# Vision tower kernel: who issues the upper halves of x's blocks 5, 6 and 7

## What is computed

```python
h = tok(x, W)              # windows of 16 steps at stride 8 (edge padding 8), rfft of each,
                           # real and imaginary parts times W: (8, 1024, 64)
f = h / norm(h)
s = softmax(f @ f.T) @ f   # over all 8192 tokens
a = f * 0.8 + s * 0.2;  a = a / norm(a)
h = layernorm(h + a)
h = layernorm(h + moe(h))  # 8 experts, the best 2 of each token, gelu: h + sum of gated experts
```

## Time and profile before

| What | Value |
|---|---|
| Time, median of 2 runs | 871.58 us (871.42 to 871.73) |
| Profiled execution: its own time | 872.53 us |
| Profiled execution: its span | 870.7 us |
| TensorE busy | 850.0 us (98%) |
| VectorE busy | 782.9 us (90%) |
| ScalarE busy | 660.2 us (76%) |
| GpSimd busy | 183.3 us (21%) |
| Mean granted TensorE clock | 0.994 |
| Moved by DMA | 26.50 MB |

### The profile page before, as it was taken

How to read it: one execution, slowest core, us unless ns; L and a number is a source line. 1 busy time by engine, 2 the same in 40 slices (tenths; PEclk the granted TensorE clock), 3 DMA queues, 4 the chain that set the end, 5 groups by cost and what they waited for, 6 DMA issues and landing times.

```text
span 870.7 us, 31169 instructions
## 1 busy us (share of the span) xinstructions
PE 850.0 (98%) x13498; PEld 438.8 (50%) x13498; DVE 782.9 (90%) x929; ACT 660.2 (76%) x1315; POOL 183.3 (21%) x187
## 2 busy tenths in 40 slices
PE   7989999999999999999999999999999999999995
PEld 6434556655555555555555555555555555543331
DVE  5677999998999899989998998899989999989994
ACT  0168888887888787878887888788878778878873
POOL 1066730000310000000000000000000299948323
PEclk9999999999999999999999999999999999999998
DMA  9984041000000000000000000000000000000111
GB/s 282 324 228 88 12 93 15 3 3 2 3 2 2 3 2 3 2 3 3 2 4 2 2 3 3 3 2 3 3 2 3 3 2 3 3 1 2 35 28 37
DMA packets 31784, 26.50 MB, mean 30 GB/s; under 512 B 12576, under 2 KB 29472, under 8 KB 31648
## 3 DMA queue, kind: packets, MB, share of 16 engines
q1 hardware_dynamic: 22768, 15.38, 7.3%
q10 hardware_dynamic: 8752, 8.86, 3.5%
q0 software_dynamic: 128, 0.26, 0.1%
HBM read 18.21 MB, written 2.10 MB: 23 GB/s over the span
## 4 chain that ended last, share of the span: by engine, by line
PE 93%; DVE 2%; ACT 2%; issue 2%; DMA 0%; POOLq 0%; DVEq 0%; ACTq 0%; POOL 0%
PE ps L532 38%; PE ps L549 26%; PE ps L562 13%; PE ps L631 3%; PE ps L714 3%; PE ps L575 2%; PE ps L449 2%; PE ps L463 1%; ACT ring L943 1%; PE ps L453 1%; PE ps L437 1%; DVE ring L1232 1%; PE ps L643 1%; PE ps L439 1%; ACT ring L906 0%
## 5 line engine op out<-in xcount | busy, mean ns | idle before, releaser
L1066 DVE TENSOR_TENSOR ring<-ring 128x1024 f16<-128x1024 f32 x512 | 605.0, 1232 | 41.1 <-ACT ring L943 40.1
L943 ACT ACTIVATE ring<-ps 128x1024 f32<-128x1024 f32 x512 | 519.7, 1021 | 128.7 <-PE ps L532 128.4
L532 PE MATMUL ps<-big 64*64 64x512 f16 x6144 | 376.3, 376 | 1.3 <-ACT ring L943 0.9
L549 PE MATMUL ps<-ring,both_f 64*64 64x512 bf16 x4096 | 275.3, 384 | 0.0
L532 PEld LDWEIGHTS ps<-big 64*64 64x64 f16 x6144 | 176.1, 106 | 159.5 <-ACT ring L943 5.5
L549 PEld LDWEIGHTS ps<-ring,both_f 64*64 64x64 f16 x4096 | 119.1, 106 | 106.8
L562 PE MATMUL ps<-ring,both_f 64*64 64x512 f16 x2048 | 154.3, 376 | 0.1
L943 ACT ACTIVATION_READ_ACCUMULATOR ring<-ps 128x1 f32 x512 | 101.2, 198 | 0.0
L376 POOL TENSOR_SCALAR stat<-stat 128x16 f32<-128x16 f32 (+2 forms) x4 | 1.9, 467 | 449.7 <-DVE stat L1115 449.4
L562 PEld LDWEIGHTS ps<-ring,both_f 64*64 64x64 f16 x2048 | 59.7, 107 | 51.9 <-issue 1.9
L906 ACT ACTIVATE ring<-ps,b1s 128x512 f32<-128x512 f32 x64 | 40.4, 683 | 17.5 <-PE ps L631 17.4
(11 more groups left out here) (181 smaller groups left out, 581.1 us busy)
## 6 DMA issues: line engine op xcount, KB each, us to landing
ring<-in_x_dram ACTq DMA_DIRECT2D x6, 1024.0 KB, 19.5
ring<-in_x_dram SPq DMA_DIRECT2D x6, 1024.0 KB, 19.9
big<-big SPq DMA_DIRECT2D x16, 128.0 KB, 2.5
out_dram<-h SPq DMA_DIRECT2D x14, 128.0 KB, 2.4
both_f<-in_x_dram SPq DMA_DIRECT2D x1, 1024.0 KB, 25.4
big<-in_x_dram SPq DMA_DIRECT2D x1, 1024.0 KB, 28.2
both_f<-in_x_dram ACTq DMA_DIRECT2D x1, 1024.0 KB, 20.6
big<-in_x_dram ACTq DMA_DIRECT2D x1, 1024.0 KB, 24.9
```

The source lines that it names most:

```text
L532: last = mm(bank(SLOT_BANK[slot_of(s)] + r)[m:m + 64, :], of_k[r][:, 128 * k + m:128 * k + m + 64], of_q[r][:, q0 + 512 * r:q0 + 512 * r + ...
L549: last = mm(bank(sums_bank(s // NT) + half)[m:m + 64, :], fs[64 * r:64 * r + 64, s % NT, m:m + 64], probs[64 * r:64 * r + 64, s % 8, :].bi ...
L943: a(probs[:, s % 8, :], bank(SLOT_BANK[slot_of(s)], 2), ACT.Exp, accum_out=rowsum[:, s:s + 1]).then_inc(s_pr, 1)
L1066: tt(probs_lo[:, s % 8, :], probs[:, s % 8, :], probs[:, s % 8, :].bitcast(BF16)[:, 1:2 * QC:2], ALU.subtract).then_inc(s_lo, 1)
```

## The change

The loop on ScalarE no longer loads blocks 5, 6 and 7. GpSimd issues these three upper halves, after its cast of `sel` and before its first inverse norm, each after the same count of `s_prod` as before. They count on three semaphores of their own, `s_xp`, since `s_xc` would otherwise be raised from two engines; the two places that wait for the upper half wait for `s_xc` (blocks 0 to 4) or `s_xp` (blocks 5 to 7), each for 16. The lower halves and all other work stay as they were.

```diff
--- before.py
+++ after.py
@@ -225,6 +225,7 @@
 
         s_cst, s_self, s_wg, s_xe, s_w, s_w1r = (sem(n) for n in ("s_cst", "s_self", "s_wg", "s_xe", "s_w", "s_w1r"))
         s_xb = [sem(f"s_x{i}") for i in range(XR)]
+        s_xp = [sem(f"s_xp{i}") for i in range(3)]
         s_xc = [sem(f"s_xc{i}") for i in range(XR)]
         s_hilo = [sem(f"s_hilo{i}") for i in range(2)]
         s_lohi = [sem(f"s_lohi{i}") for i in range(2)]
@@ -327,6 +328,10 @@
             nc.gpsimd.tensor_copy(ident16[:, :], ident).then_inc(s_id16, 1)
             pool.wait_ge(s_self, 32)
             nc.gpsimd.tensor_copy(sel[:, :], sel_f).then_inc(s_id16, 1)
+            for b in X_BEHIND:
+                pool.wait_ge(s_prod, X_BEHIND[b])
+                pool.dma_start(x_at(b)[64:128, 0:NM].rearrange("p m s v -> p m (s v)"),
+                               x_h[b, 1]).then_inc(s_xp[b - 5], 16)
             gt, pool_ts = nc.gpsimd.tensor_tensor, nc.gpsimd.tensor_scalar
 
             def sl(n):
@@ -456,7 +461,7 @@
 
             def loaded(b):
                 pe.wait_ge(s_xb[X_SLOT[b]], 16 * X_TURN[b])
-                pe.wait_ge(s_xc[X_SLOT[b]], 16 * X_TURN[b])
+                pe.wait_ge(s_xc[b] if b < 5 else s_xp[b - 5], 16)
 
             def kept_busy(n):
                 for i in range(n):
@@ -803,9 +808,6 @@
                 edge(b)
             for b in range(B):
                 act.wait_ge(s_prod, b + 1)
-                for later in X_BEHIND:
-                    if X_BEHIND[later] == b + 1:
-                        load(later)
                 used = 12 if b >= 2 else 8
                 a(prod[:, b // 2, 0:used, b % 2, :], bank(2 * (b % 2), 2)[:, 0:V * used].rearrange("p (k v) -> p k v", v=V),
                   ACT.Copy).then_inc(s_prodev, 1)
@@ -1015,7 +1017,7 @@
 
                 if s == SHARED_TAPS[b][0]:
                     dve.wait_ge(s_xb[X_SLOT[b]], 16 * X_TURN[b])
-                    dve.wait_ge(s_xc[X_SLOT[b]], 16 * X_TURN[b])
+                    dve.wait_ge(s_xc[b] if b < 5 else s_xp[b - 5], 16)
                     dve.wait_ge(s_edge, b - 1)
                 if (b - 1, s) in SHARED:
                     dve.wait_ge(s_taken, SHARED.index((b - 1, s)) + 1)
```

## The result

The changed kernel takes 884.89 us (median of 2 runs, 884.64 to 885.15), the kernel before 871.58. The ratio is 1.0154, with a 95% interval of 1.0137 to 1.0170: 13.3 us slower. The profiled execution took 885.15 us at a span of 883.3. The forecast was slower by 4.6 us, 876.2, with a range of 868.5 to 880. The direction was right and so was the place, the landing of block 4; the forecast loss was a third of what came, and the time lies above the range.

The account below looks back on a forecast made before the run. TensorE bounds the steady part; in the head, ScalarE's issue stalls delay block 4. Crowding by GpSimd's packets would start block 4 at 50.4 instead of 45.79, clock unchanged: 871.6 + 4.6 = 876.2 us, range 868.5 to 880.

Parts of the forecast that it names:

- What bounds the head, and the stall: First 75 us: ScalarE's 5.79 us issues delay block 4; removal worth 3.8 + 1.75 = 5.5 us if x were there.
- 0.3 for block 5: Block 5 landing at 47.4 against 47.1 wanted would take back at most 0.3 us of the gain.
- GpSimd's issues and the cover behind them: GpSimd's three issues take 1.7 us each; even at 5.79, the delayed inverse norm is barely covered by ScalarE's 2.88 us idle.
- The packets: Queues alternate by packet; GpSimd's 4 KB against 1 KB take two thirds of the rate, starting 4.8 us after issue.
- The landing of block 4: GpSimd's 3.15 MB pass first at 348 GB/s, 9.0 us: block 4 lands at 50.4, starting 4.6 us late.
- the loads behind block 4: After 50.4, block 5's lower half needs 3.0 us at 348 GB/s, landing at 53.4; nothing else is late.
- The fifth rival: Slow clock lasts through blocks 4 and 5, or one 1 KB-packet queue misses 348 GB/s: above 880 us; chance 0.06.
- The clock: TensorE around block 4: same 1.75 us slow-clock cost as before, no difference; bounds a gain or loss of 1.75.
- No crowding: GpSimd's packets of x do not hold up block 4; the 5.5 us less 0.3 is gained: 866.4 us; chance 0.13.
- equal shares: GpSimd's packets of x are 1 KB, each queue gets 116 GB/s, block 4 lands at 44.5: 869.8 us; chance 0.13.
- the stall only moves: GpSimd's queue fills, its issues take 5.79 us or more and delay the inverse norms: 871.6 us; chance 0.06.

Follow-up runs that it names:

- in another way: Kernel before, with ScalarE issuing block 6's half behind its b = 1 copies and block 7's behind the squares of h 0 and 1: 867.65 us, 0.9944.
- The transfers alone: Separate kernel, computing nothing of the reference: only loads of x in eleven successive phases, varying queues and partition halves; 204 to 213 GB/s into one half, 347 to 351 into both.
- the run with blocks 6 and 7: Changed kernel, but GpSimd issues only the upper halves of blocks 6 and 7 and ScalarE block 5's: 879.78 us, 1.0086 of the kernel before.
- the one with SyncE alone: Changed kernel, but SyncE instead of GpSimd issues the upper halves of blocks 5 to 7, each behind its lower half: 880.07 us, 1.0090 of the kernel before.
- the ninth phase: Phase of the loads-only kernel with SyncE loading the lower half, ScalarE and GpSimd the upper, the changed kernel's mix: 253 GB/s.
- the fifth phase: Phase of the loads-only kernel with GpSimd alone loading the upper half of the partitions: 213 GB/s.

## Why the prediction was right or wrong

**What bounds the head, and the stall: right.** The issues of 5.79 us were the chain, and taking them off ScalarE in another way brings 4.9 us of the 5.5 worked out; 0.3 for block 5 had been foreseen, block 7's 0.74 us had not.

**GpSimd's issues and the cover behind them: right.** Taken at 1.7 us each, they were 0.82 to 0.88. The inverse norm stands at 45.21, no later than the 45.97 of the earlier trace rows.

**The packets: right.** From the stretch in the earlier trace rows the prediction took the turn by packets, the 4 KB, the two thirds, and the start 4.8 us after the issue. All came: the first of GpSimd's packets of x are seen from 35.5 us on, 4.6 us after the issue at 30.87, and it moved 2.87 of 4.23 MB between 36 and 54 us, 68%.

**The landing of block 4: the step that failed.** "... all 3.15 MB pass ahead of block 4's end, and at 348 GB/s that is 9.0 us. Block 4 lands at 41.4 + 9.0 = 50.4." It landed at 58.7. The rate of 348 GB/s is the term that was wrong. The 3.15 MB did pass ahead, but at a total of 235 GB/s: 4.23 MB in the 18 us from 36 to 54. At that rate GpSimd's share is 0.16 MB per us, so its halves need 19.7 us instead of 13.6, and the other queues get 42 and 33 GB/s where 58 had been taken for each. The engines' total of 348 is a sum over two halves of the partitions, and the change put two of three queues, with five parts of six of the bytes, into one of them. The transfers alone show this cap, the run with blocks 6 and 7 shows that it gives the right landing, and the one with SyncE alone that it holds without GpSimd. By that GpSimd would be through at 35.5 + 19.7 = 55.2, and it was: 3.13 MB by 55.5. The last 3 us are the cap once more. ScalarE's queue has next to nothing left, and SyncE's stands nearly alone with the lower half (queues from 55.5 to 58.5 us):

```profile
q1 hardware_dynamic: 555, 0.57, 109.1%
```

That is 190 GB/s again. Some of these bytes were already block 5's: from 38.6, when block 3's half had landed, to 58.7 SyncE's queue moved 1.43 MB, where block 4's half is 1.05. A half lands in sixteen parts (its semaphore rises by 16), and in the trace's semaphore events those of block 4 lie far apart, 44.3 to 57.4 us for the upper half and 51.1 to 58.7 for the lower, where before both lay between 38.3 and 41.4. The wait ends with the last part. Why the parts drift so far apart stays open.

The same 348 was taken for the loads behind block 4, 3.0 us for each lower half. SyncE's queue alone moved 191 GB/s (1.52 MB from 62 to 70 us), so block 5's landed 5.5 us behind block 4's, at 64.2. Here that cost no more than the 0.31 us of wait, since VectorE wanted it 5.1 us after block 4.

The trace of before had a warning. It is in a half microsecond of the edge loads a little behind the one that the prediction read (DMA queues, 19.0 to 19.5 us):

```profile
DMA packets 64, 0.13 MB, mean 252 GB/s; under 512 B 1, under 2 KB 44, under 8 KB 64
...
q0 software_dynamic: 21, 0.08, 70.0%
q10 hardware_dynamic: 22, 0.02, 21.3%
```

There the total is 252 GB/s with the same packets in turn, and over both edge loads, 18 to 20 us, it is 244. The prediction took the one stretch at full rate, 352, for the rule, and put no bound on the rate itself. The later stretch shows the rate lower, not why. The one that it took was a start: in the changed kernel too the first half microsecond with GpSimd's packets, 35.5 to 36, has 385 GB/s, and what follows has 235. The fifth rival had "a single queue of 1 KB packets doesn't reach 348 GB/s", with the wrong cause: it was the half, not the queue (348 from one queue into 128 partitions).

**The clock: right in result.** TensorE lost the upper level as before, with 14 us of idle as with 2.85. It lost it at another moment: during the idle (PEclk 0.50 from 50 us on) and not 1.4 us after work had begun again, at 48.5. It worked about 3 us at the lower level in both. The assumed difference was none; measured are 4.31 against 4.33 us for the two slow taps.

**The rivals.** No crowding and equal shares fall with the packets. That the stall only moves falls with GpSimd's short issues. The fifth, above 880, had a chance of 0.06 and took in the time that came, but neither of its causes was the one at work: the slow clock lasted no longer than before, and the late landings behind block 4 cost 0.31 us.

## What to carry to other kernels

Before an issue moves to another engine, ask what it stood behind in its old queue: that order was a priority, and here the late blocks were let past the urgent one, with packets four times as large. Count bytes per half of the partitions as well as in total, and keep both halves busy at any time, with transfers into all 128 partitions or with two queues in step. If an issue holds its engine for microseconds, first move the issue behind the work that others wait for, on the same engine: here that brought 4.9 us, and the move to another queue cost 13.3.

## What the runs showed of the hardware

- Transfers from DRAM in runs of 1 KB reached 204 to 213 GB/s into partitions 0 to 63 or 64 to 127 alone, from one queue or two, and 347 to 351 into both. SyncE's and GpSimd's queues were alike in this; ScalarE's wasn't measured alone. In the kernel SyncE's queue, alone in one half, moved 186 to 194 GB/s.
- Beside two queues of 1 KB packets, GpSimd's took two thirds of the rate, in 4 KB packets, also where the runs are 1 KB (0.66 of 1.00 MB in the ninth phase).
- The first packets of a GpSimd issue came 4.6 to 4.8 us after it beside busy queues, 7.3 us with three issues in a row (43.49 to 50.8); with idle queues, in the fifth phase of the transfers alone, GpSimd issued at 67.10 and its first packets are seen between 68.5 and 69 us.
- A DMA issue of 1 MiB on ScalarE took 0.57 us (block 5, before) to 7.84 us (block 4, changed kernel). The long ones came with more of its transfers still on their way; that a full queue is what holds the engine is inferred from this. On GpSimd it took 0.82 to 0.88 us each time, three deep.
